# Means and variances of four layer norms made on GpSimd, half of the rows at a time, instead of on VectorE

## The reference

```
h = (x - mean(x)) / sqrt(var(x) + 1e-5) * (1 + ca) + sa
x = x + ga * attention0(h)         # causal, scores of 1024 x 1024, one head
h = layernorm(x) * (1 + cb) + sb
x = x + gb * experts(h)            # softmax gate, 1 of 8 experts a row
# the second layer, with its own weights and modulations
h = layernorm(x) * (1 + ca) + sa
x = x + ga * attention1(h)         # 16 heads of 8 channels, all rows
h = layernorm(x) * (1 + cb) + sb
x = x + gb * (two linear layers without an activation)
```

## Time and profile before

| | |
|---|---|
| median of 3 runs | 1774.61 us (1774.03 to 1776.43) |
| the profiled execution, own time | 1779.59 us |
| its span, first to last instruction | 1778.3 us |
| busy: PE, DVE, ACT, POOL | 1671.1, 1507.9, 1378.1, 731.7 us |
| mean granted TensorE clock | 0.988 |

### The profile page before, as it was taken

The page is one execution under the profiler, slowest core; times in us unless marked ns, Lnnn a source line. Parts: engine busy times, 40 slices in busy tenths (PEclk is TensorE's granted clock), DMA queues, the critical chain, the costliest instruction groups (busy, mean ns, idle before and its releaser), DMA issues.

```text
span 1778.3 us, 54970 instructions
## 1 busy us (share of the span) xinstructions
PE 1671.1 (94%) x23327; PEld 659.4 (37%) x23337; DVE 1507.9 (85%) x2321; ACT 1378.1 (77%) x1934; POOL 731.7 (41%) x1195
## 2 busy tenths in 40 slices
PE   5777999999999999999999999999999999999998
PEld 2542333334333343334333343333433343222224
DVE  4669888898888988899888988899888998999973
ACT  4442678887798778887798877987788877887885
POOL 2321356435544465344654265434654355211110
PEclk9988899999999999999999999999999999999999
DMA  2130111112220322012211222103211122201101
GB/s 71 50 110 24 58 50 58 35 58 55 80 71 14 96 70 72 29 43 74 80 52 34 62 59 87 56 23 91 67 59 36 37 73 71 70 23 50 35 28 34
DMA packets 97233, 99.95 MB, mean 56 GB/s; under 512 B 11116, under 2 KB 81436, under 8 KB 96988
## 3 DMA queue, kind: packets, MB, share of 16 engines
q1 hardware_dynamic: 96188, 95.66, 17.9%
q10 hardware_dynamic: 800, 0.79, 0.1%
HBM read 61.02 MB, written 34.57 MB: 54 GB/s over the span
## 4 chain that ended last, share of the span: by engine, by line
PE 67%; DVE 15%; ACT 13%; issue 3%; DMA 1%; POOL 0%; ACTq 0%; SPq 0%; DVEq 0%
PE pv_psum L818 23%; PE side_psum L551 15%; PE buffer L802 12%; PE buffer L792 10%; DVE row_max L1328 8%; ACT p L1028 7%; PE side_psum L641 2%; PE buffer L551 2%; PE side_psum L608 1%; ACT o_sb L1037 1%; DVE s L1175 1%; ACT s L946 1%; DVE st_f L1087 1%; ACT s L939 1%; ACT hT_b L1017 1%
## 5 line engine op out<-in xcount | busy, mean ns | idle before, releaser
L1328 DVE TENSOR_REDUCE row_max<-buffer 128x2 f32<-128x1024 f32 x1024 | 1234.8, 1219 | 158.7 <-PE buffer L792 145.8
L1028 ACT ACTIVATE p<-buffer 128x1024 f32<-128x1024 f32 x1024 | 1047.5, 1025 | 209.5 <-PE buffer L802 193.6
L818 PE MATMUL pv_psum<-p,v 128*9 128x256 f32 x8192 | 583.9, 381 | 5.8 <-ACT o_sb L1037 5.2
L792 PE MATMUL buffer<-k_ops,q_ops 48*128 48x512 bf16 x2048 | 396.3, 384 | 18.5 <-ACT p L1028 8.8
L802 PE MATMUL buffer<-q_ops,k_ops 51*128 51x512 bf16 x2048 | 400.7, 388 | 6.9 <-DVE row_max L1328 5.8
L818 PEld LDWEIGHTS pv_psum<-p,v 128*9 128x9 f32 x8192 | 149.8, 89 | 316.6 <-issue 233.9
L802 PEld LDWEIGHTS buffer<-q_ops,k_ops 51*128 51x128 bf16 x2048 | 98.2, 93 | 372.0 <-issue 227.7
L1461 POOL TENSOR_TENSOR hm<-masks,hT_f 128x1024 f32<-128x1024 bf16 x56 | 120.3, 2149 | 107.5 <-PE side_psum L551 107.5
L792 PEld LDWEIGHTS buffer<-k_ops,q_ops 48*128 48x128 bf16 x2048 | 99.4, 94 | 117.4 <-ACT p L1028 99.4
L1476 POOL TENSOR_SCALAR nm_parts<-nm 128x16 bf16<-128x16 f32 x64 | 16.2, 253 | 270.4 <-DVE nm L1253 269.9
L551 PE MATMUL side_psum<-we,hm 128*32 128x128 f32 x3648 | 121.0, 274 | 0.0
(11 more groups left out here) (297 smaller groups left out, 1665.1 us busy)
## 6 DMA issues: line engine op xcount, KB each, us to landing
masks<-masks_rows SPq DMA_DIRECT2D x16, 1024.0 KB, 5.8
q_ops<-products SPq DMA_DIRECT2D x128, 96.0 KB
k_ops<-products SPq DMA_DIRECT2D x128, 96.0 KB
products<-q_parts SPq DMA_DIRECT2D x16, 384.0 KB, 2.6
products<-k_parts SPq DMA_DIRECT2D x14, 384.0 KB, 2.8
attention<-o_sb SPq DMA_DIRECT2D x248, 18.0 KB
x<-in_L_attn_inputs SPq DMA_DIRECT2D x8, 512.0 KB, 4.2
products<-q_parts SPq DMA_DIRECT2D x16, 256.0 KB, 3.0
```

The lines of the kernel that those rows point to most:

```text
L792: m = e.matmul(buffer[:, hh, :], q_ops[rows_of(hh, K_MAX), slot, of, i * P:(i + 1) * P], k_ops[rows_of(hh, K_MAX), slot, of, halves(half)[ ...
L818: m = e.matmul(pv_psum[q:q + VW, half * QUARTER:(half + 1) * QUARTER], v1[b % 2][:, kb, 2 * hp + hh, :], p_sb[n % KEPT][:, hh, part * QUAR ...
L1028: e.activation(p_sb[n % KEPT][:, :, :], unit("exp", n)[0][:, :, :], ACT.Exp).then_inc(S["exp_done"], 1)
L1328: e.tensor_reduce(mx[pair % 2][:, :, i, half], unit("max", n)[0][:, :, :], axis=AX.X, op=ALU.max).then_inc(S["max_done"], 1)
```

## The change

`bn_aggr` is left out of `norm_stats` (but for the three norms of batch 0 and the first norm of batch 1, `in_lone_part`). POOL's `norm_small` reads the six numbers of `bn_stats` itself and makes from them, on four tiles at a time, minus the mean (half the sum of the two means), and four times the variance + eps; since the power then is half of what it was, `modT`'s scale is doubled. `norm_small` takes eight instructions, four of them followed by a wait, where it took three with one. DVE gets waits, so that it doesn't overwrite `st` before POOL has read it.

```diff
+def in_lone_part(b, which):
+    return b == 0 or (b, which) == (1, 0)
...
-        def norm_stats(src, st, mv, half, part, signal):
+        def norm_stats(src, st, mv, half, part, signal, alone=False):
             for t in two(half, part):
                 m = e.bn_stats(st[:, t, :], src[:, t, :])
-            after(m)
-            for t in two(half, part):
-                m = e.bn_aggr(mv[:, t, :], st[:, t, :])
+            if alone:
+                after(m)
+                for t in two(half, part):
+                    m = e.bn_aggr(mv[:, t, :], st[:, t, :])
...
                 dve.wait_ge(S[f"x2_{half}"], b + 1)
+                dve.wait_ge(*norm("small", b, 1, half))
+            elif b:
+                dve.wait_ge(*norm("small", b - 1, 2 * which, half))
...
-            e.tensor_scalar(modT[:, l, 1::2, :], view[:, 1::2, :], 1.0, None, ALU.add).then_inc(S["mod"], 1)
+            e.tensor_scalar(modT[:, l, 1::2, :], view[:, 1::2, :], 1.0, 2.0, ALU.add, ALU.mult).then_inc(S["mod"], 1)
...
+            dve.wait_ge(S["small_b"], 2 * (b - 1) + half + 1)
             norm_stats(xs[b % 4], st_b, mv_b, half, part, S["stats_b"])
...
-        def norm_small(mv, sm, half, signal):
+        def norm_small(st, mv, sm, half, signal, alone=False):
             tiles = halves(half)[0]
-            e.tensor_scalar(sm[:, 0, tiles], mv[:, tiles, 0], -1.0, 0.0, ALU.mult, ALU.add)
-            after(e.tensor_scalar(sm[:, 1, tiles], mv[:, tiles, 1], 1.0, EPS, ALU.mult, ALU.add))
+            if alone:
+                e.tensor_scalar(sm[:, 0, tiles], mv[:, tiles, 0], -1.0, 0.0, ALU.mult, ALU.add)
+                after(e.tensor_scalar(sm[:, 1, tiles], mv[:, tiles, 1], 4.0, 4 * EPS, ALU.mult, ALU.add))
+            else:
+                after(e.tensor_tensor(mv[:, tiles, 0], st[:, tiles, 1], st[:, tiles, 4], op=ALU.subtract))
+                e.tensor_tensor(sm[:, 0, tiles], st[:, tiles, 1], st[:, tiles, 4], op=ALU.add)
+                e.tensor_tensor(sm[:, 1, tiles], st[:, tiles, 2], st[:, tiles, 5], op=ALU.add)
+                after(e.tensor_tensor(mv[:, tiles, 1], mv[:, tiles, 0], mv[:, tiles, 0], op=ALU.mult))
+                e.tensor_scalar(sm[:, 0, tiles], sm[:, 0, tiles], -0.5, 0.0, ALU.mult, ALU.add)
+                after(e.tensor_scalar(sm[:, 1, tiles], sm[:, 1, tiles], 4.0 / C, 4 * EPS, ALU.mult, ALU.add))
+                after(e.tensor_tensor(sm[:, 1, tiles], sm[:, 1, tiles], mv[:, tiles, 1], op=ALU.add))
             e.tensor_tensor(sm[:, 2, tiles], sm[:, 1, tiles], minus_half[:, tiles], op=ALU.pow).then_inc(signal, 1)
```

More of the change, by code:

```diff
@@ L1107, in stats @@
                 dve.wait_ge(S[f"x2_{half}"], b + 1)
+                dve.wait_ge(*norm("small", b, 1, half))
+            elif b:
+                dve.wait_ge(*norm("small", b - 1, 2 * which, half))
             st, mv = (st_f, mv_f) if which else (st_attn, mv_attn)
-            norm_stats(xs[b % 4], st, mv, half, part, norm("stats", b, which, half)[0])
+            norm_stats(xs[b % 4], st, mv, half, part, norm("stats", b, which, half)[0], in_lone_part(b, which))
         def apply(b, which, half):
@@ L1372, in stats @@
             pool.wait_ge(*(norm("xn", b, 1, half) if which == 2 else norm("xn", b - 1, 2 * which, half)))
-            mv, sm = (mv_f, sm_f) if which else (mv_attn, sm_attn)
-            norm_small(mv, sm, half, norm("small", b, which, half)[0])
+            st, mv, sm = (st_f, mv_f, sm_f) if which else (st_attn, mv_attn, sm_attn)
+            norm_small(st, mv, sm, half, norm("small", b, which, half)[0], in_lone_part(b, which))
         def apply(b, which, half):
@@ L1512, in stats_b @@
             pool.wait_ge(S["stats_b"], 2 * b + half + 1)
-            norm_small(mv_b, sm_b, half, S["small_b"])
+            norm_small(st_b, mv_b, sm_b, half, S["small_b"])
         def apply_b(b, half):
```

## The result

The changed kernel takes 1784.26 us (median of 5 runs, 1781.47 to 1785.69), the kernel before 1776.43 us beside it (5 runs). The ratio is 1.0035, 95% interval 1.0022 to 1.0049: **slower by 6.2 us (3.9 to 8.7)**. The two medians are 7.8 us apart, which this interval takes in; the text goes by the ratio. The forecast was a loss of 11.7 us and 1786.3 us; the direction and the places were right, the size was too large. That 1784.26 us lies so near 1786.3 is in part luck: the kernel before measured 1.8 us above the 1774.61 us from which the forecast started.

A forecast was written before the change was run, and what follows sets the result against it. PE was taken as the bound (busy 94%, 67% of the chain), DVE paying only on the chain. 9.6 + 5.3 - 2.8 - 0.5 - 0.8 + 0.95 = +11.7 us on 1774.61 gave 1786.3 us; 8-in-10 range 1774 to 1800.

The forecast's parts named there:

- A call longer by 1.36 us: In norm_small on POOL: seven instructions instead of two ahead of the power, which begins 1.36 us later in each call.
- A: Half 0 of the third norm, batches 2 to 7: PE's transposes wait 1.6 us for xn_f, six times, +9.6 us.
- B: Half 1 of the third norm, batches 1 to 7: xn_f and PE's transposes later by 0.75 us, seven times, +5.3 us.
- C: Half 1 of the second norm, batches 1 to 7: DVE's shorter quarters gain some 0.4 us, seven times, -2.8 us.
- Half 0 of the second norm: Taken at 0: PE asks for the result later than its end by more than the delay.
- Single places and tail: Quarters in batch 1 at 135 to 138 us -0.5, near 1635 us -0.8; batch 7's last norm +0.95 us.
- What costs nothing: Places taken as hidden, such as the first norm, hm, x_wff, the parts, DVE's added waits and the doubled scale: 0.
- (1): Rival: POOL's longer call stays hidden everywhere, so the kernel is faster by 6.8 us, 1767.8 us; chance 0.10.
- (2): Rival: calls grow by about 0.8 us and nothing measurable changes, -1.1 us, 1773.5 us; chance 0.12.
- (3): Rival: POOL is slower, 0.5 us a step, possibly by strided reads of st; +59 us, 1833 us; chance 0.04.
- (4): Rival: the forecast's loss, and PE's pauses also lower its granted clock, 1792 to 1798 us; chance 0.11.
- (5): Rival: DVE was the true bound and eight on-chain quarters a batch gain 0.27 us each, -15, 1760 us; chance 0.03.

The follow-up runs named there:

- e3: The change applied only to the third and fourth norms, the other norms as in the kernel before: 1785.95 us, ratio 1.0051.
- e10: The change's long POOL call only for half 0 of the third norm, all else aggregated on DVE: 1778.4 us, ratio 1.0007.
- e11: The change's long POOL call only for the fourth norm, the other norms aggregated on DVE: 1775.75 us, ratio 0.9992.
- e4: The change with POOL's eight instructions, but DVE aggregates as before too, its result unused: 1796.8 us, ratio 1.0112.
- e5: The change without DVE's aggregations, but POOL makes only three instructions, on even channels' statistics, so it computes something else: 1769.78 us, ratio 0.9962.
- e2: The change applied only to norms 0 and 1, the third and fourth as in the kernel before: 1772.14 us, ratio 0.9974.
- e1: The change with all norms aggregated on DVE again, keeping only DVE's new waits and the doubled scale: 1776.93 us, ratio 1.0001.
- e6: The change with one instruction less in POOL's call and waits placed behind independent instructions: 1775.88 us, ratio 0.9998.
- e9: The shortened call of e8 for norms 0, 1 and the fourth, the third norm as in the kernel before: 1770.69 us, ratio 0.9964.
- e8: The shortened call of e6 with the factor -0.5 applied by a TENSOR_TENSOR instead of a TENSOR_SCALAR: 1774.89 us, ratio 0.9989.

## Why the prediction was right, and where its sizes were off

- **A call longer by 1.36 us.** 1.16. The steps that are followed by a wait were right (0.27 to 0.30 for 0.28). Of the others, two start 0.15 to 0.16 after the one before, not 0.26, since they don't wait for each other and overlap (845.42, 845.58, 845.73). This term alone makes the sum too large: with 1.16 in the forecast's own formulas A is 1.2 and B 0.59.
- **A, +9.6.** +6.3. Mechanism and number of places are right (e3, e10, e11). By the scores it is 6 x 1.13 = 6.8, next to the 1.20 of the formula; the rest of 0.1 is C's.
- **Batch 1 at A, 0.** PE waits 0.35 there for `xn_f` (0.37 in e10, 0.90 in e4). The forecast took 0 without working it out, and by its own sign a new wait at such a place speaks against it; C in batch 1 has another, 0.36. What it costs can't be read, as it is within the first 236 us.
- **B, +5.3.** +3.7. The 1.6 us of DVE's quarters are not to be had: e5 measures 0.1.
- **C, -2.8.** -2.5 at the transposes, -3.2 by the scores, in six batches; the seventh can't be read. The 0.4 a batch came out by luck. By the forecast's own times `xn_f` ends at 797.34 and PE starts at 797.45 or 797.48, which leaves 0.2 or 0.25 of the 0.54, not 0.4. With the 1.16 that the call really grew it would be 797.14 + 0.14 = 797.28, which leaves 0.42. And the lateness that was taken off is not paid at all, as the scores behind the transposes show: that term should have been the full 0.54.
- **Half 0 of the second norm, 0.** -0.14 in each of six batches, -0.8 in all, in the change and in e2. In just these two the custom DVE instruction on `s` that runs beside `xn_f` (L1184, 758.74 after) starts 0.49 behind the start of `xn_f` and takes 1.08 us; before, and in e1, e3 and e5 to e11, it starts 0.59 behind it and takes 1.23 (L1175, 761.20 before). PE's wait for ACT a little later shrinks from 0.50 to 0.35. In e4 the instruction takes 1.09 too, with a step of -0.04 only, so it is not shown to be the cause.
- **Single places and tail.** Near 1635 us -0.76 for -0.8; the tail +0.7 for +0.95. The 0.5 us at 135 us can't be read for the clock.
- **What costs nothing.** Right for the waits and the scale (e1), and for x_wff, the parts and the fourth norm: no other transposes fall behind by more than 0.02 at a place.
- **DVE's busy time, -37 forecast.** -21.5. The 0.165 us of a `bn_aggr` can't be multiplied by 224: the rows of a pair overlap. The groups by line show it, 128 of them busy for 15.9 us, 0.124 each; after, `mv_f` has 16 with 2.0, and no `mv_b` any more. 27.7 us of groups went, and `row_max` has 5.1 more. This changed no term of the sum, which used 0.25 for a pair.
- **Rivals.** (1) and (2) need a call that grows by less than 0.56 or by 0.8. e6, at 0.78, is rival 2 come true: forecast -1.1, measured -0.4. (3) did not occur: the strided reads of `st` take 0.20 to 0.21 at A, B and C (0.28 once, in the tail). (4) did not show: the granted clock is 1.00 from 670 to 880 us in the change and in e4, which has the longest pauses, and the means over the span are 0.987 and 0.986 (0.988 before). Its reading of the page was loose: the slices with an 8 in the clock line have 7, 7 and 9 tenths of PE's time busy, and the first slice, with 5, has a 9. (5) is ruled out by e5.

The group on `mv_f` that is left on DVE (groups by line: busy us, mean ns | idle before):

```profile
L1096 DVE BATCH_NORM_AGGREGATE mv_f<-st_f 128x2 f32<-128x6 f32 x16 | 2.0, 166 | 0.3
```

The Trainium skill (GPSIMD Engine Reference, § 4.1 Engine selection) has GpSimd about 2 times slower in two-input operations. One such operation stands on both engines in this kernel, the masked copy `hm`, and there the trace comes near the page, with a factor of 1.7 (groups by line, after):

```profile
L1482 POOL TENSOR_TENSOR hm<-masks,hT_f 128x1024 f32<-128x1024 bf16 x56 | 120.4, 2150 | 107.6 <-PE side_psum L556 107.6
L1248 DVE TENSOR_TENSOR hm<-masks,hT_f 128x1024 f32<-128x1024 bf16 x8 | 9.9, 1238 | 6.8 <-PE buffer L556 4.5 <-ACT hT L917 2.3
```

At 4 elements no operation stands on both. A TENSOR_TENSOR takes 0.20 to 0.21 us on POOL and a `bn_aggr` 0.165 on DVE, but these are different operations, so the row that the forecast held against the ratio does not test it. What did not come is the 0.33 plus 0.08 us a step that the forecast worked out by it: at A the steps took 0.15 to 0.30. The call became slow by the number of its instructions and their waits (1.16 us more on POOL for two pairs of 0.25 less on DVE), and that is what PE waited for.

## What to carry to other kernels

Moving work to an idle engine is priced place by place by the slack of its result: here a call of GpSimd that was 1.16 us longer cost nothing, 0.3 or 1.2 us, by how many of them stood in a row ahead of a waiting TensorE. Split such a change by its places and keep it where the giving engine is on the chain and the taking one has slack: the same edit made e2 4.6 us faster and, used everywhere, the kernel 6.2 us slower; with a shorter call on the right places (e9) it was 6.4 us faster. To know which parts count, hold the starts of the same instruction in both traces against each other: steps of 0.05 us can be read there, where single runs scatter by 5 us and more. Take more than one instruction for it: the transposes at C are 0.1 late, the scores behind them are not.

## What the hardware showed unexpectedly

- Small GpSimd instructions that don't wait for each other start 0.15 to 0.16 us apart while each is busy for 0.20 to 0.21; with a wait on the one before it is 0.27 to 0.30. But not every gap follows that rule: two without a wait between them stand 0.26 (L1375 to L1376) and 0.28 (e8, L1376 to L1377) apart. What decides that is open.
- While a DVE TENSOR_SCALAR runs, two of the same small GpSimd instructions are busy for 0.28 and 0.30 us instead of 0.20, and the call (1770.97 to 1772.84) takes 1.87 instead of 1.70. e3, e4 and e11 show the same 0.28 and 0.30 at this place. No run takes the DVE instruction away, so that it is the cause is not shown. In the last norm after (timeline of POOL and DVE):

```profile
1771.03 1.12 DVE L1104 TENSOR_SCALAR xn_b<-x,sm_b 128x128 f32<-128x128 f32 x4 [1.36 <-POOL sm_b L1379]
1771.25 0.21 POOL L1372 TENSOR_TENSOR sm_b<-st_b 128x4 f32<-128x4 f32 x1
1771.41 0.28 POOL L1373 TENSOR_TENSOR sm_b<-st_b 128x4 f32<-128x4 f32 x1
1771.65 0.30 POOL L1374 TENSOR_TENSOR mv_b<-mv_b 128x4 f32<-128x4 f32 x1
```

- Two instructions that overlap seem to trade time: `xn_f` on POOL (four instructions) takes 2.56 us where the custom DVE instruction beside it takes 1.23, and 2.66 where that takes 1.08. Each kernel has one of the two pairs, within 0.02, in all six batches; what picks between them is open.

- The granted clock falls to 0.83 in one stretch of 10 us near the end in two of the profiles (the change, e10) and not in the others, in the same code; it costs 1.5 us in the execution that has it.
